# The exponentials of a graph attention kernel written twice by ScalarE: into PSUM for the weighting, into SBUF for the sums

## The chip, the cores and the metric

The kernel runs on one core of one Trainium2 chip. The metric is device time in microseconds (us). Three runs of the kernel before took 1232.32, 1234.52 and 1235.27 us; the median is 1234.52 us.

## What is computed

One graph attention layer with residual and layer norm, over 6250 nodes of 96 features, 4 heads of 24, and 106,250 edges (100,000 drawn ones in both directions and the self loops), sorted by destination. `src` plays the rows, `dst` the columns.

```python
q = (embeds[rows] @ qW).reshape(e, 4, 24)
k = (embeds[cols] @ kW).reshape(e, 4, 24)
v = (embeds[cols] @ vW).reshape(e, 4, 24)
exp_s = exp(clip(einsum('ehd,ehd->eh', q, k), -10, 10))
norms = segment_sum(exp_s, rows)[rows]
res = segment_sum(exp_s / (norms + 1e-8) * v, rows)
x = layernorm(x + x + res)
```

## The kernel before

**Set-up.** The nodes form 49 blocks of 128. x is transposed and multiplied by the three weights; k and v of every node go to a table in HBM (kv_table, 192 floats a row), q stays in SBUF (qt).

**Edges.** The edges are sorted by block on the chip, in 6 groups. After each group VectorE writes the list of table rows to gather (`dst_s`, line 1159) and the place of each edge in its block (`loc_s`). Sorted edges form 880 columns of 128, and five columns (U = 5) make a tile, so there are 176 tiles. Ten of them share their gathered rows in pairs, so GpSimd gathers for 171.

**A tile n** passes through these steps:
- GpSimd issues five indirect DMAs (line 511) that gather k and v into `kv`, a ring of eight buffers. Before a tile it waits until the ring's buffer is free (`s_wv` of tile n-8) and until the sums of tile n-6 are made (`s_res`).
- VectorE builds the one-hot matrix `ohb` (line 1191). TensorE transposes it ("t", line 679), ScalarE copies the transpose to `onehT` (line 776) and the matrix itself to `oneh` (line 782).
- TensorE multiplies `onehT` with q's block into the PSUM tensor `ps_q[n % 2]` ("q", line 653): q of each edge, 480 of 512 columns.
- VectorE multiplies with k ("prod", line 1202), reduces over 24 (line 1222) and clips (line 1230). ScalarE takes the exponential, 20 values a partition, into `wv[..., 96:100]` (line 769).
- VectorE multiplies v with these, each broadcast over 24, into `wv[..., 0:96]` ("wv", line 1212).
- TensorE multiplies `oneh` with the 100 columns of `wv` into `ps_r` ("r", line 667), and VectorE adds the five results to `acc` (line 1183): the weighted v and, in the last four columns, the sums of weights.

**Order.** A plan written at build time (`plan`) strings these steps together. Every engine walks it in the same order, one iteration m at a time, with work of several tiles in each, and each engine's queue is strictly in order. In iteration m:
- TensorE: q of tile m+1, r of tile m-1, t of tile m+2, then matmuls of the sort (a "unit" is 20 matmuls, line 636, one unit behind VectorE's, or the matmuls of a named piece, as `tally` at line 563 or `table` at lines 578 to 583).
- VectorE: prod of tile m, wv of tile m-1, then, once r of tile m-2 is there, the five additions of tile m-2, interleaved with reduce, build of tile m+2 and clip, then sort work.
- ScalarE: the first part of a unit's steps (line 728), the exponential of tile m, `onehT` of tile m+2, `oneh` of tile m+1 (after r of tile m-1), the other part of the steps.

Sort work of group g runs inside the iterations of group g-1's tiles. For each group VectorE ranks the edges first (`mark`, `tally`, `pair`, `count`, `base`, `bounds`, `select`, `table`, `tree`, with matmuls of tally, count and table between), then runs the units, and then a short end (`lower`, `differ`, `turn`, `choice`, `pick`), which crosses TensorE, ScalarE and VectorE several times. `pick` writes `dst_s`, for which GpSimd waits before the first tile of the group. After the last group there is no sort work. Then come the division, the residual, the layer norm and the stores.

**Waits that the change touches.** q of tile n waits for `onehT` of n and, since `ps_q` has two buffers, for prod of tile n-2:

```python
pe.wait_ge(s_oneT, n + 1)
wait(pe, s_prod, n - 1)
```

r of tile n waits for `wv` (`s_wv`), for `oneh` (`s_onf`) and for the additions of tile n-2.

Of the kernel before, what the change touches and what calls it, by code (L numbers as in the profile page):

```python
# [6 lines left out]
def gnn(nc, x, src, dst, qW, kW, vW, out):  # L7
# [3 lines left out]
    ACT = mybir.ActivationFunctionType  # L11
    AX = mybir.AxisListType

    P = 128
    N, D = x.shape
    E = src.shape[0]
    HEADS = 4
    DH = D // HEADS
# [4 lines left out]
    RW = D + HEADS  # L23
    U = 5
# [52 lines left out]
    def gathered(n):  # L77

        if not isinstance(n, int) or n >= MB + MT // U:
            return n - PAIRS // U  # L80
        return n if n < MB else MB + (n - MB) // 2
# [68 lines left out]
    with ExitStack() as ctx:  # L150
        def sb(name, shape, dt):
            return ctx.enter_context(nc.sbuf_tensor(name, shape, dt))

        def pb(name, shape, dt):
            return ctx.enter_context(nc.psum_tensor(name, shape, dt))

        def sem(name):
            return ctx.enter_context(nc.semaphore(name))
# [106 lines left out]
        clipped = sb("clipped", [P, 2, U * HEADS], f32)  # L265
        wv = sb("wv", [P, 2, U, RW], f32)
# [31 lines left out]
        ps_q = [pb(f"ps_q{i}", [P, 512], f32) for i in range(2)]  # L298
# [56 lines left out]
        s_prod = sem("s_prod")  # L355
        s_score = sem("s_score")
        s_clip = sem("s_clip")
        s_exp = sem("s_exp")
        s_wv = sem("s_wv")
        s_res = sem("s_res")  # L360
        s_acc = sem("s_acc")
# [12 lines left out]
        def wait(eng, s, v):  # L374

            if not (isinstance(v, int) and v <= 0):
                eng.wait_ge(s, v)
# [37 lines left out]
        def sums_of(g):  # L415

            return (ps_a, ps_b) if g == 0 else (ps_a[:, 0:256], ps_a[:, 256:512])

        def there(n):

            return not isinstance(n, int) or 0 <= n < NBT

        def blocks_of(engine, n):

            return nc.values_load_multi_w_load_instructions(  # L425
                blk_s[0:1, bass.ds(n * U, U)], engines=[engine], min_val=0, max_val=NB - 1,
                skip_runtime_bounds_check_because="clamped when the table is made")[1]
# [98 lines left out]
        def _(pe):  # L526
# [96 lines left out]
            def unit(g, v, vm):  # L623
                w = TS[g] + 1
                first = isinstance(v, int) and v == V0[g]
                last = isinstance(v, int) and v == V0[g + 1] - 1
                if first:
                    pe.wait_ge(s_blk, g + 1)
                pe.wait_ge(s_theta, v + 1)
                for to, lhs, s_made in zip(sums_of(g), (lhs_a, lhs_b), (s_lhs_a, s_lhs)):  # L630
                    pe.wait_ge(s_made, v + 1)
                    for j in range(SU):
                        steps = theta[:, vm, j, 0:w]
                        if j < (KG if g else KD):
                            steps = theta_g[:, vm, 0:w, j] if g else theta_d[:, vm, :, j]
                        mm = nc.tensor.matmul(to[:, 0:w], lhs[:, vm, :, j], steps,  # L636
                                              start=first and j == 0 and (g == 0 or lhs is lhs_a),
                                              stop=last and j == SU - 1 and (g == 0 or lhs is lhs_b))
                    if last and lhs is lhs_a:
                        mm.then_inc(s_half, 1)  # L640
                mm.then_inc(s_bin, 1)

            def tiles(m, mm, sorts, mid=()):
                n, nm = m + 1, (mm + 1) % R
                if there(n):

                    blks = blocks_of(mybir.EngineType.PE, n)
                    if isinstance(n, int) and n == 0:
                        pe.wait_ge(s_qi, NPC)
                    pe.wait_ge(s_oneT, n + 1)  # L650
                    wait(pe, s_prod, n - 1)
                    for u in range(U):
                        last = nc.tensor.matmul(ps_q[nm % 2][:, u * D:(u + 1) * D],  # L653
                                                onehT[:, nm % 2, u * P:(u + 1) * P],
                                                qt[:, bass.ds(blks[u], 1), :].rearrange("p a d -> p (a d)"),
                                                start=True, stop=True)
                    last.then_inc(s_q, 1)
                n, nm = m - 1, (mm - 1) % R
                if there(n):

                    pe.wait_ge(s_wv, n + 1)
                    pe.wait_ge(s_onf, n + 1)
                    wait(pe, s_acc, U * (n - 1))
                    for u in range(U):
                        final = isinstance(n, int) and n == NBT - 1
                        to = ps_last[u][:, 0:RW] if final else ps_r[nm % 2][:, u * RW:(u + 1) * RW]
                        last = nc.tensor.matmul(to, oneh[:, nm % 2, u, :], wv[:, nm % 2, u, :],  # L667
                                                start=True, stop=True)
                        if final:
                            last.then_inc(s_last, 1)  # L670
                    if not final:
                        last.then_inc(s_res, 1)
                n, nm = m + 2, (mm + 2) % R
                if there(n):

                    pe.wait_ge(s_one, n + 1)
                    wait(pe, s_oneT, n - 1)
                    for u in range(U):
                        last = nc.tensor.transpose(ps_t[nm % 2][:, u * P // 2:(u + 1) * P // 2].bitcast(bf16),  # L679
                                                   ohb[:, nm % 4, :, u], ident_bf[:, :])  # L680
                    last.then_inc(s_ot, 1)
                for piece, g in mid:
                    piece(g)
                for sort in sorts:
                    unit(*sort)
# [6 lines left out]
        def _(act):  # L692
# [70 lines left out]
            def tiles(m, mm, sorts, mid=()):  # L763
                if sorts:
                    unit(*sorts[0], halves=(0,))
                n, nm = m, mm
                if there(n):
                    act.wait_ge(s_clip, n + 1)
                    nc.scalar.activation(wv[:, nm % 2, :, D:RW],  # L769
                                         clipped[:, nm % 2, :].rearrange("p (u h) -> p u h", h=HEADS),  # L770
                                         ACT.Exp).then_inc(s_exp, 1)
                n, nm = m + 2, (mm + 2) % R
                if there(n):
                    wait(act, s_q, n - 1)
                    act.wait_ge(s_ot, n + 1)
                    nc.scalar.activation(onehT[:, nm % 2, :], ps_t[nm % 2][:, 0:U * P // 2].bitcast(bf16),  # L776
                                         ACT.Copy).then_inc(s_oneT, 1)
                n, nm = m + 1, (mm + 1) % R
                if there(n):
                    wait(act, s_res, n - 1)  # L780
                    act.wait_ge(s_one, n + 1)
                    nc.scalar.activation(oneh[:, nm % 2, :, :], ohb[:, nm % 4, :, :].rearrange("p n u -> p u n"),  # L782
                                         ACT.Copy).then_inc(s_onf, 1)
                if sorts:
                    unit(*sorts[0], halves=(1,))
                for piece, g in mid:
                    piece(g)
                for sort in sorts[1:]:
                    unit(*sort)
# [12 lines left out]
            for j, (a, b) in enumerate(PARTS):  # L802
                act.wait_ge(s_inv, j + 1)
                for i in range(a, min(b, NPC - 1)):
                    for k in range(PC if i < NPC - 2 else HALF):
                        if j + 1 < len(PARTS) and i == b - 1 and k == (PC - 2 if b < NPC - 2 else 2):
                            root(j + 1)
                        n = i * PC + k
# [6 lines left out]
        def _(dve):  # L815
# [356 lines left out]
            def tiles(m, mm, sorts, mid=()):  # L1172
# [33 lines left out]
                def weigh():  # L1206
                    n, nm = m - 1, (mm - 1) % R
                    if there(n):

                        km = (gathered(n) if isinstance(n, int) else nm - PAIRS // U) % R  # L1210
                        dve.wait_ge(s_exp, n + 1)
                        nc.vector.tensor_tensor(  # L1212
                            wv[:, nm % 2, :, 0:D].rearrange("p u (h d) -> p u h d", h=HEADS),
                            kv[:, km, :, D:2 * D].rearrange("p u (h d) -> p u h d", h=HEADS),
                            wv[:, nm % 2, :, D:RW].unsqueeze(3).to_broadcast([P, U, HEADS, DH]),
                            ALU.mult).then_inc(s_wv, 1)

                def reduce():
# [117 lines left out]
            for k in range(HALF, PC):  # L1336
                n = (NPC - 2) * PC + k
# [3 lines left out]
            n = (NPC - 1) * PC  # L1341
# [31 lines left out]
```

## Time and profile before

| what | us |
|---|---|
| median of three runs | 1234.52 |
| the profiled execution, own time | 1236.72 |
| its span, first to last instruction | 1234.9 |
| VectorE busy | 1036.8 (84%) |
| TensorE busy | 967.6 (78%) |
| GpSimd busy | 861.0 (70%) |
| ScalarE busy | 613.4 (50%) |

Busy time leaves out what an engine's sequencer does, such as issuing, waiting and branching. The column behind the bar in a row of costliest groups is the busy time and the mean of one; behind the second bar stands the idle time of that engine just before these instructions and what ended it. "Issue" means that the profile shows nothing that was waited for. In a timeline a row has its start, its duration, engine, line, operation and the tiles written and read; in brackets the idle time of the engine before it and what ended it. TensorE's granted clock was 0.754 of full speed on average.

### The profile page before, as it was taken

Reading aid. Unit: us, or ns where it says so; the run is one execution under the profiler, and the core shown is the slowest. Engines: PE = TensorE matmul, PEld = TensorE weight load, DVE = VectorE, ACT = ScalarE, POOL = GpSimd, SP = SyncE. Lnnn points to the kernel's source line nnn. Section 1 sums busy time; section 2 is a strip of 40 time slices with the busy share of each in tenths; the row PEclk is TensorE's granted clock in tenths of the full one; section 3 lists DMA queues with packets and bytes.
Section 4 is the critical chain, followed back from the end, with each engine's and each line's share of the span. In section 5 each row is a group of like instructions: output and inputs, shape, how many; then the busy total and the mean of one; then the engine's idle time right before and its main releaser. Section 6 shows DMA issues by size and latency. Waiting matters only on the chain.

```text
span 1234.9 us, 22885 instructions
## 1 busy us (share of the span) xinstructions
PE 967.6 (78%) x6512; PEld 881.1 (71%) x6513; DVE 1036.8 (84%) x3109; ACT 613.4 (50%) x1328; POOL 861.0 (70%) x888
## 2 busy tenths in 40 slices
PE   8875788688886888768998868978777788888770
PEld 6764777587775887667887767877677677777760
DVE  7989899999999999989999998999667855555557
ACT  6851583258732598323887323877333422222225
POOL 1207777777777777777777777777777777777752
PEclk9996597769976699865999855999767955555555
DMA  6202222223222222232222222222522222222222
GB/s 177 90 3 76 80 78 71 75 78 80 78 72 77 78 78 78 74 81 75 78 78 78 71 74 79 78 78 78 154 77 80 78 80 77 80 77 79 78 58 78
DMA packets 67240, 98.33 MB, mean 80 GB/s; under 512 B 33127, under 2 KB 53204, under 8 KB 67134
## 3 DMA queue, kind: packets, MB, share of 16 engines
q0 software_dynamic: 41040, 84.10, 25.1%
q1 hardware_dynamic: 26094, 12.94, 3.7%
q8 instruction: 51, 0.84, 0.3%
q14 instruction: 55, 0.45, 0.1%
HBM read 89.77 MB, written 7.22 MB: 79 GB/s over the span
## 4 chain that ended last, share of the span: by engine, by line
DVE 35%; POOL 22%; PE 18%; issue 17%; DVEq 4%; ACT 3%; DMA 0%; POOLq 0%; ACTq 0%
POOL kv L511 22%; DVE acc L1183 7%; PE ps_r L667 5%; PE ps_q L653 4%; DVE place_m L1119 4%; DVEq L425 4%; DVE prod L1202 3%; DVE place_m L1123 3%; DVE wv L1212 3%; PE ps_a L636 2%; DVE steps_m L872 1%; PE ps_t L679 1%; PE ps_a L563 1%; DVE place_m L1071 1%; PE ps_r L548 1%
## 5 line engine op out<-in xcount | busy, mean ns | idle before, releaser
L511 POOL DMA_INDIRECT kv<-kv_table,dst_s x855 | 840.0, 982 | 306.9 <-issue 299.0
L653 PE MATMUL ps_q<-qt,onehT 128*128 x1760 | 319.2, 347 | 99.5 <-ACT onehT L776 95.5
L667 PE MATMUL ps_r<-wv,oneh 128*128 128x100 f32 x1752 | 325.7, 352 | 90.9 <-DVE wv L1212 90.2
L653 PEld LDWEIGHTS ps_q<-qt,onehT 128*128 128x128 f32 x1760 | 291.5, 254 | 123.5 <-issue 123.4
L667 PEld LDWEIGHTS ps_r<-wv,oneh 128*128 128x128 f32 x1752 | 296.2, 259 | 112.1 <-DVE wv L1212 109.5
L728 ACT ACTIVATE steps_m<-iota_f,pos_t 125x254 f16<-125x254 f32 (+4 forms) x652 | 255.8, 479 | 13.1 <-PE ps_b L636 8.8
L1183 DVE TENSOR_TENSOR acc<-acc,ps_r 128x100 f32 x876 | 221.9, 253 | 41.9 <-issue 12.9
L776 ACT ACTIVATE onehT<-ps_t 128x640 f32<-128x640 bf16 x176 | 123.8, 704 | 209.3 <-PE ps_t L679 202.1
L769 ACT ACTIVATE wv<-clipped 128x20 f32<-128x20 f32 x176 | 38.5, 219 | 344.6 <-DVE clipped L1230 340.0
L1202 DVE TENSOR_TENSOR prod<-ps_q,kv 128x480 f32<-128x480 f32 x176 | 114.9, 653 | 111.2 <-DMA kv<-kv_table,dst_s 100.7
L782 ACT ACTIVATE oneh<-ohb 128x640 f32<-128x640 bf16 x176 | 164.2, 933 | 0.8 <-PE ps_r L667 0.8
L636 PE MATMUL ps_a<-steps_m,place_m 125*128 125x254 f16 (+4 forms) x1220 | 152.8, 268 | 0.0
L636 PEld LDWEIGHTS ps_a<-steps_m,place_m 125*128 125x128 f16 x1220 | 134.0, 139 | 1.9
L1222 DVE TENSOR_REDUCE score<-prod 128x20 f32<-128x480 f32 x176 | 113.9, 647 | 4.9 <-PE ps_r L667 2.5
L1212 DVE TENSOR_TENSOR wv<-kv,wv 128x480 f32<-128x480 f32 x176 | 114.3, 650 | 2.5 <-issue 2.2
L679 PE MATMUL ps_t<-ident_bf,ohb 128*128 128x128 bf16 x880 | 103.1, 264 | 8.8 <-DVE ohb L1191 8.2
L679 PEld LDWEIGHTS ps_t<-ident_bf,ohb 128*128 128x128 bf16 x880 | 87.0, 138 | 18.7 <-DVE ohb L1191 17.4
L1191 DVE TENSOR_TENSOR ohb<-iota_t,loc_s 128x640 bf16<-128x640 bf16 x176 | 97.6, 554 | 0.0
L636 PE MATMUL ps_a<-theta_g,place_m 125*128 125x254 f16 (+3 forms) x284 | 56.5, 280 | 16.8 <-ACT steps_m L728 16.8
L1123 DVE TENSOR_TENSOR place_m<-place_m,ps_b 125x1280 f16<-125x1280 f16 x71 | 57.8, 815 | 0.2
L1126 DVE TENSOR_TENSOR place_m<-place_m,ps_b 125x1280 f16<-125x1280 f16 x71 | 57.8, 814 | 0.0
L1119 DVE TENSOR_TENSOR place_m<-iota_s,ps_b 125x1280 f16<-125x1280 f16 x71 | 57.8, 814 | 0.0
(214 smaller groups left out, 691.2 us busy)
## 6 DMA issues: line engine op xcount, KB each, us to landing
kv<-kv_table,dst_s POOLq DMA_INDIRECT x855
kv_table<-kv SPq DMA_DIRECT2D x7, 672.0 KB, 3.4
acc<-in_x_dram SPq DMA_DIRECT2D x6, 336.0 KB, 6.6
steps_m<-in_x_dram SPq DMA_DIRECT2D x6, 336.0 KB, 5.3
out_dram<-kv SPq DMA_DIRECT2D x6, 336.0 KB
dst_i<-in_dst_dram SPq DMA_DIRECT2D x1, 415.0 KB
src_i<-in_src_dram SPq DMA_DIRECT2D x1, 346.7 KB
acc<-in_x_dram SPq DMA_DIRECT2D x1, 288.0 KB, 4.4
```

What stands on the lines that cost most here:

```text
L511: nc.gpsimd.indirect_dma_start(kv[:, nm, u, :], None, kv_dram, bass.IndirectOffsetOnAxis(ap=dst_s[:, n * U + u:n * U + u + 1], axis=0)).th ...
L636: mm = nc.tensor.matmul(to[:, 0:w], lhs[:, vm, :, j], steps, start=first and j == 0 and (g == 0 or lhs is lhs_a), stop=last and j == SU - ...
L653: last = nc.tensor.matmul(ps_q[nm % 2][:, u * D:(u + 1) * D], onehT[:, nm % 2, u * P:(u + 1) * P], qt[:, bass.ds(blks[u], 1), :].rearrange ...
L667: last = nc.tensor.matmul(to, oneh[:, nm % 2, u, :], wv[:, nm % 2, u, :], start=True, stop=True)
L679: last = nc.tensor.transpose(ps_t[nm % 2][:, u * P // 2:(u + 1) * P // 2].bitcast(bf16), ohb[:, nm % 4, :, u], ident_bf[:, :])
L728: last = nc.scalar.activation(theta[:, vm, j, 0:w], iota_f[0:EP, 0:w], ACT.Sign, scale=-1.0, bias=pos_t[:, bass.ds(v * SU + j, 1)])
L776: nc.scalar.activation(onehT[:, nm % 2, :], ps_t[nm % 2][:, 0:U * P // 2].bitcast(bf16), ACT.Copy).then_inc(s_oneT, 1)
L782: nc.scalar.activation(oneh[:, nm % 2, :, :], ohb[:, nm % 4, :, :].rearrange("p n u -> p u n"), ACT.Copy).then_inc(s_onf, 1)
L1183: nc.vector.tensor_tensor(at, at, from_ps, ALU.add).then_inc(s_acc, 1)
L1202: nc.vector.tensor_tensor(prod[:, nm % 2, :].rearrange("p (u d) -> p u d", u=U), ps_q[nm % 2][:, 0:U * D].rearrange("p (u d) -> p u d", u= ...
L1212: nc.vector.tensor_tensor(wv[:, nm % 2, :, 0:D].rearrange("p u (h d) -> p u h d", h=HEADS), kv[:, km, :, D:2 * D].rearrange("p u (h d) -> ...
L1222: nc.vector.tensor_reduce(score[:, nm % 2, :], prod[:, nm % 2, :].rearrange("p (h d) -> p h d", d=DH), axis=AX.X, op=ALU.add).then_inc(s_s ...
```

## The change

ScalarE's exponential now writes 20 values a partition into the 32 spare columns of the tile's own `ps_q` buffer, and VectorE's weighting reads them there. A second exponential of the same clipped scores, placed on ScalarE's queue behind the copy to `onehT`, writes `wv[..., 96:100]` as before and has its own semaphore `s_sum`. As the weights lie in the buffer that q of tile n+2 overwrites, q of tile n no longer waits for prod of tile n-2 but for wv of tile n-2. r waits for `s_sum` too.

```diff
+        def weights(nm):
+
+            return ps_q[nm % 2][:, U * D:U * D + U * HEADS].rearrange("p (u h) -> p u h", h=HEADS)
...
                     pe.wait_ge(s_oneT, n + 1)
-                    wait(pe, s_prod, n - 1)
+                    wait(pe, s_wv, n - 1)
...
                     pe.wait_ge(s_wv, n + 1)
+                    pe.wait_ge(s_sum, n + 1)
                     pe.wait_ge(s_onf, n + 1)
...
                     act.wait_ge(s_clip, n + 1)
-                    nc.scalar.activation(wv[:, nm % 2, :, D:RW],
+                    nc.scalar.activation(weights(nm),
                                          clipped[:, nm % 2, :].rearrange("p (u h) -> p u h", h=HEADS),
                                          ACT.Exp).then_inc(s_exp, 1)
...
                     nc.scalar.activation(onehT[:, nm % 2, :], ps_t[nm % 2][:, 0:U * P // 2].bitcast(bf16),
                                          ACT.Copy).then_inc(s_oneT, 1)
+                n, nm = m, mm
+                if there(n):
+                    nc.scalar.activation(wv[:, nm % 2, :, D:RW],
+                                         clipped[:, nm % 2, :].rearrange("p (u h) -> p u h", h=HEADS),
+                                         ACT.Exp).then_inc(s_sum, 1)
...
                             kv[:, km, :, D:2 * D].rearrange("p u (h d) -> p u h d", h=HEADS),
-                            wv[:, nm % 2, :, D:RW].unsqueeze(3).to_broadcast([P, U, HEADS, DH]),
+                            weights(nm).unsqueeze(3).to_broadcast([P, U, HEADS, DH]),
                             ALU.mult).then_inc(s_wv, 1)
```

## Rows read from the trace of the kernel before

**Rows 1.** The page, costliest groups: gather, prod, wv, exponential.

```profile
L511 POOL DMA_INDIRECT kv<-kv_table,dst_s x855 | 840.0, 982 | 306.9 <-issue 299.0
L1202 DVE TENSOR_TENSOR prod<-ps_q,kv 128x480 f32<-128x480 f32 x176 | 114.9, 653 | 111.2 <-DMA kv<-kv_table,dst_s 100.7
L1212 DVE TENSOR_TENSOR wv<-kv,wv 128x480 f32<-128x480 f32 x176 | 114.3, 650 | 2.5 <-issue 2.2
L769 ACT ACTIVATE wv<-clipped 128x20 f32<-128x20 f32 x176 | 38.5, 219 | 344.6 <-DVE clipped L1230 340.0
```

**Rows 2.** Instructions of tile dst_s: shortest, median, longest in ns; first, last start.

```profile
L511 POOL DMA_INDIRECT kv<-kv_table,dst_s x855: 940/946/2863, 90.0 to 1194.2; - x171
```

**Rows 3.** Timeline of GpSimd: gathers of tiles 17, 39 and 50.

```profile
202.24 0.94 POOL L511 DMA_INDIRECT kv<-kv_table,dst_s  x1 [2.88 <-DVE dst_s L1159]
...
345.61 1.09 POOL L511 DMA_INDIRECT kv<-kv_table,dst_s  x1 [2.21 <-PE ps_r L667]
...
417.26 0.94 POOL L511 DMA_INDIRECT kv<-kv_table,dst_s  x1 [0.82 <-issue]
```

**Rows 4.** Timeline of GpSimd and VectorE: gathers begun while VectorE works.

```profile
112.44 1.09 POOL L511 DMA_INDIRECT kv<-kv_table,dst_s  x1 [0.30 <-issue]
...
273.08 0.81 DVE L1126 TENSOR_TENSOR place_m<-place_m,ps_b 125x1280 f16<-125x1280 f16 x1
...
273.58 0.94 POOL L511 DMA_INDIRECT kv<-kv_table,dst_s  x1 [0.30 <-issue]
...
723.28 0.65 DVE L1212 TENSOR_TENSOR wv<-kv,wv 128x480 f32<-128x480 f32 x1
723.42 1.32 POOL L511 DMA_INDIRECT kv<-kv_table,dst_s  x1 [0.30 <-issue]
...
1102.39 1.02 POOL L511 DMA_INDIRECT kv<-kv_table,dst_s  x1 [0.30 <-issue]
```

**Rows 5.** Timeline at the table of group 1: q, wv, r, then VectorE's read.

```profile
124.81 2.45 PE L653 MATMUL ps_q<-qt,onehT 128*128 x10 [0.94 <-ACT onehT L776]
...
127.03 0.65 DVE L1212 TENSOR_TENSOR wv<-kv,wv 128x480 f32<-128x480 f32 x1
127.73 2.46 PE L667 MATMUL ps_r<-wv,oneh 128*128 128x100 f32 x10 [0.48 <-DVE wv L1212]
...
131.36 0.26 DVE L997 CAST blk_s<-ps_a 1x110 int32<-1x110 f32 x1 [2.38 <-PE ps_a L583]
```

**Rows 6.** The same read of groups 2 and 4.

```profile
253.90 0.28 DVE L997 CAST blk_s<-ps_a 1x125 int32<-1x125 f32 x1
...
570.08 0.31 DVE L997 CAST blk_s<-ps_a 1x160 int32<-1x160 f32 x1 [0.75 <-PE ps_a L583]
```

**Rows 7.** Timeline at the last unit of group 1.

```profile
187.02 1.36 PE L667 MATMUL ps_r<-wv,oneh 128*128 128x100 f32 x10 [0.94 <-DVE wv L1212]
...
188.39 0.47 PE L679 MATMUL ps_t<-ident_bf,ohb 128*128 128x128 bf16 x5
...
192.38 0.40 PE L636 MATMUL ps_a<-theta_g,place_m 125*128 125x205 f16 x2 [1.70 <-ACT steps_m L728]
...
195.61 0.66 DVE L1202 TENSOR_TENSOR prod<-ps_q,kv 128x480 f32<-128x480 f32 x1
```

**Rows 8.** Timeline: VectorE at the start of group 1's units.

```profile
149.41 0.37 DVE L1115 TENSOR_TENSOR theta_g<-iota_g,ps_b 125x410 f16<-125x410 f16 x1 [1.45 <-PE ps_a L636]
```

**Rows 9.** Timeline: prod of tile 64, behind the tally of group 4.

```profile
527.15 0.66 DVE L1202 TENSOR_TENSOR prod<-ps_q,kv 128x480 f32<-128x480 f32 x1 [1.44 <-PE ps_q L653]
```

**Rows 10.** Timeline: r of tile 70, and the gather of tile 76.

```profile
580.56 2.46 PE L667 MATMUL ps_r<-wv,oneh 128*128 128x100 f32 x10 [0.85 <-DVE wv L1212]
...
585.51 0.95 POOL L511 DMA_INDIRECT kv<-kv_table,dst_s  x1 [0.30 <-issue]
```

**Rows 11.** Timeline after the last group: q of tile 146, prod of tile 145.

```profile
1005.89 2.45 PE L653 MATMUL ps_q<-qt,onehT 128*128 x10 [0.88 <-ACT onehT L776]
...
1006.81 0.66 DVE L1202 TENSOR_TENSOR prod<-ps_q,kv 128x480 f32<-128x480 f32 x1 [1.98 <-DMA kv<-kv_table,dst_s]
```

More of the change, by code:

```diff
@@ L358, in gnn @@
         s_exp = sem("s_exp")
+        s_sum = sem("s_sum")
         s_wv = sem("s_wv")
```

## The prediction

> **What bounds the kernel now.** Read the page's costliest groups first: VectorE has the most busy time, but GpSimd's 855 gathers have 840.0 us busy and 299.0 us idle put down to issue [rows 1], 1139 us in a span of 1234.9. The tile view says that they run from 90.0 to 1194.2 us [rows 2]: 1104 us over 855 is 1.29 us each, and one alone takes 0.946 (median) and 0.30 of issue, 1.25. So GpSimd is never idle for long, and the end comes with its last gather. Then read GpSimd's timeline for every pause above 0.30 us. After 90 us there are three [rows 3]: at 202.24 for the sorted list of group 1 (from VectorE), at 345.61 and at 417.26 for r of the tile six before (from TensorE). So GpSimd sets the time, but VectorE's sort and TensorE's r come just in time up to 417 us: what delays them there delays GpSimd. Behind the last group VectorE waits for gathers instead [rows 11].
>
> **The part that gains: wv no longer has two inputs in SBUF.** 855 x (982 - 946) ns = 31 us of the gathers is lengthening [rows 1, 2]. Look at what VectorE did when a long one began: wv started at 723.28, a gather at 723.42, wv ended at 723.93 and the gather 0.81 us later, at 724.74 [rows 4]. All 52 gathers that begin well inside a wv are lengthened so; of 202 that begin inside prod, the reduction or the unit's products, which have at most one SBUF input, 201 are not, as the one inside line 1126 with its PSUM operand [rows 4]. Counting the ones that a wv lengthens by over 15 ns gives 57, first at 112.44 and last at 1102.39 [rows 4], together 10.1 us, of which 4.8 us after 585 us. This goes. (The building of ohb does the same, 11.4 us, and stays.) [...]
>
> **wv's own duration.** No row shows wv with weights in PSUM. Nearest is prod, same size with one PSUM input: 653 ns against 650 [rows 1]. Bounds: 176 x 3 ns = +0.5 us, and at best the few tens of ns by which VectorE itself waits when a gather began first, -1 us. I take 0.
> [...]
>
> **The exponential.** The one into PSUM replaces one of 219 ns [rows 1]. ScalarE writes no PSUM in the trace, so the bounds are 0 and the 933 ns of its longest regular copy; VectorE's wait before wv is 2.5 us in all [rows 1], and wv follows prod, so nothing shows at either but the high end. I take 219. The second costs 176 x 219 ns = 38.5 us of ScalarE, which idles 344.6 us before exponentials alone: 0, except where `oneh` behind it is urgent (below). s_sum comes before the next q starts, so r never waits for it.
>
> **The part that costs: q waits for wv of two tiles before.** Today q of tile m+1 runs far ahead, during VectorE's previous iteration: q at 124.81, while the wv that it will have to follow is at 127.03 and ends at 127.68 [rows 5]. [...] q itself still comes in time for its prod. What is late next, place by place up to 585 us:
> - Table. VectorE waits at 131.36 for matmuls that follow wv, r, t without a gap, 2.38 us idle already [rows 5]: +2.45. There are four such places, groups 1 to 4, the second and the last in [rows 6]; at the second VectorE is just not idle, so up to 0.1 less. 9.7 us.
> - First units of group 1: VectorE waits 1.45 us for TensorE's units [rows 8], and these follow r. The clock rises inside them, so between 1.3 and 2.0; I take 1.4.
> - Last unit of groups 1, 2, 3: r 187.02, t 188.39, onehT, oneh, five steps on ScalarE, units 192.38, then q, on which prod at 195.61 waits [rows 7]. It is one unbroken chain: +1.27 for q and +0.22 for the second exponential ahead of oneh. 3 x 1.49 = 4.5 us.
> - Tally of group 4: prod of tile 64 already waits 1.44 us for a q that stands behind the tally [rows 9], and the tally behind r: +2.4.
> - The ends of the groups and the other iterations: q is still there before its prod, and r before its additions. 0.
>
> VectorE is then 9.7 + 1.4 + 4.5 + 2.4 = 18.0 us late at 585 us.
> GpSimd: its first gather of tile 76 starts at 585.51, and the one before ended at 585.21 [rows 10]. It needs r of tile 70, which ended at 580.56 + 2.46 = 583.02 [rows 10], 2.2 us earlier; a wait for r ends some 0.5 us behind the modelled end (as before 417.26), so 1.7 us are spare. r moves by VectorE's 18.0 and by q's 2.45 in front of it: 18.0 + 2.45 - 1.7 = +18.8 us for GpSimd. What the freed port gave before that is lost, since GpSimd waits here anyway; so is a lower sum at the earlier places (tile 17: 2.45 + 1.4 + 1.49 = 5.3; tile 50: 5.3 + 3.8 + 2.4 + 2.45 = 14). Behind 585 us there is no pause for GpSimd to the end, and the lists of groups 4 and 5 come well ahead of their first gather: only the port counts, -4.8.
> Behind the last group the order costs nothing: TensorE's round q, r, t, copy, q takes 6.1 to 6.3 us, it waits 0.88 in it for the copy, and prod waits 1.98 us for its gather [rows 11]; only the phase moves.
>
> **Sum.** Against the profiled execution, 1236.72 us of its own (span 1234.9, 1.8 around it): 1236.7 + 18.8 - 4.8 = 1250.7. That execution lies 2.2 above the median 1234.52, so 1248.5; I say 1248. Ends: the four table places may cost 1.3 each where the clock is at its upper level, and r the same, 6 us less; each place where TensorE has spare time that I did not see takes 1 to 2 off; on the other side the skipped ends of groups (4 of them at 1 to 1.5) and a dearer wv add 6. Own range 1239 to 1256.
>
> **Rivals.**
> - The port gain carries through: q is early by microseconds today, so its new wait costs nothing, and all 10.1 us go from a bound engine: 1224. For it: GpSimd is busy throughout [rows 2], and q starts before wv in every row. Against: what counts is not q, but r and the table behind it [rows 5]. Not slower; it decides if TensorE has 2.5 us spare behind wv. 7%.
> - Partly absorbed: a VectorE delay of 18 us is taken up by spare time, the first pauses [rows 3] cost about 5 us and the port gives 5 back: 1235. For it: VectorE idles 2.38, 1.45 and 1.44 us at these very places. Against: it idles because of TensorE, so this idle time moves along. 10%.
> - [...] 11%.
> - That the change does not do what it says (r or the sums waiting elsewhere) I see no way for.
>
> **From cases to numbers.** Main case 72%: 1248. A difference of 0.3%, 3.7 us, is what a measurement of this kernel can tell from none. Faster by more: 8% (the first rival and a rest). Within: 10%. Slower: 82%. The range for 8 in 10 takes the main case's and part of the second and third rival: 1236 to 1258.
>
> **What would show it.** In the trace after: gathers inside a wv at 0.95 us; q's matmuls starting within 0.1 us behind wv, TensorE's waits for wv in front of q and no longer in front of r; VectorE's idle time before the table's read near 4.8 us for group 1; GpSimd's pauses in front of tiles 17, 24 to 28, 39, 45 to 51 and 71 to 76, some 19 us more in all; wv at 650 ns. I am wrong if r follows wv at once, if those pauses are missing, or if wv is above 700 ns.

## The result, and the profile after

The changed kernel takes 1248.96 us (median of 5 runs, 1246.27 to 1250.0) where the kernel before, on the same chip, took 1235.27 (5 runs): a ratio of 1.012, 95% interval 1.010 to 1.014. So it is 14 us slower; 1248 was forecast. The profiled execution took 1248.96 us of its own, span 1247.1.

The groups of the page after, in the columns of [rows 1]:

```profile
L516 POOL DMA_INDIRECT kv<-kv_table,dst_s x855 | 827.3, 968 | 332.6 <-issue 320.2
L658 PE MATMUL ps_q<-qt,onehT 128*128 x1760 | 318.9, 345 | 245.4 <-DVE wv L1223 211.1
...
L673 PE MATMUL ps_r<-wv,oneh 128*128 128x100 f32 x1752 | 309.7, 342 | 2.6 <-DVE wv L1223 2.6
...
L1213 DVE TENSOR_TENSOR prod<-ps_q,kv 128x480 f32<-128x480 f32 x176 | 114.8, 652 | 105.8 <-DMA kv<-kv_table,dst_s 91.5
...
L775 ACT ACTIVATE ps_q<-clipped 128x20 f32<-128x20 f32 x176 | 32.7, 186 | 169.2 <-DVE clipped L1241 169.0
L1223 DVE TENSOR_TENSOR wv<-kv,ps_q 128x480 f32<-128x480 f32 x176 | 113.3, 644 | 2.6 <-issue 2.2
```

Read it against [rows 1]. The gathers got shorter, 968 ns from 982, which is 12.7 us less busy time, but GpSimd's idle time grew by more. TensorE's 211.1 us of waiting for wv now stands in front of q; before, 90.2 us of it stood in front of r (row below). Now r waits 2.6 us in all, because what it needs is there by the time that q has passed. wv takes 644 ns.

```profile
L667 PE MATMUL ps_r<-wv,oneh 128*128 128x100 f32 x1752 | 325.7, 352 | 90.9 <-DVE wv L1212 90.2
```

GpSimd's tile view [rows 2] says what that makes at the end: the last gather starts 12.3 us later, though the first starts 0.8 us earlier.

```profile
L516 POOL DMA_INDIRECT kv<-kv_table,dst_s x855: 940/946/2142, 89.2 to 1206.5; - x171
```

What the text calls the port gain is only this: wv no longer lengthens gathers. No run shows a port; the word is the author's name for the effect. In the timeline after, a gather that starts inside a wv takes 0.95 us, where [rows 4] had 1.02 to 1.32.

```profile
111.27 0.64 DVE L1223 TENSOR_TENSOR wv<-kv,ps_q 128x480 f32<-128x480 f32 x1
111.65 0.95 POOL L516 DMA_INDIRECT kv<-kv_table,dst_s  x1 [0.30 <-issue]
```

The table of group 1, against [rows 5]: q starts 0.25 us behind wv's end (within 0.1 was forecast), not before wv, r comes 2.2 us after q's start, and VectorE's idle time before its read has gone from 2.38 to 4.70.

```profile
126.16 0.64 DVE L1223 TENSOR_TENSOR wv<-kv,ps_q 128x480 f32<-128x480 f32 x1
...
127.05 2.44 PE L658 MATMUL ps_q<-qt,onehT 128*128 x10 [1.78 <-DVE wv L1223]
...
129.28 2.35 PE L673 MATMUL ps_r<-wv,oneh 128*128 128x100 f32 x10
...
132.79 0.26 DVE L1008 CAST blk_s<-ps_a 1x110 int32<-1x110 f32 x1 [4.70 <-PE ps_a L588]
```

And GpSimd's pauses. Before there were three [rows 3]; now there are 21, the last in front of tile 76. Some of them, in GpSimd's timeline (the number in brackets is the pause):

```profile
172.66 0.94 POOL L516 DMA_INDIRECT kv<-kv_table,dst_s  x1 [1.15 <-issue]
...
186.98 0.94 POOL L516 DMA_INDIRECT kv<-kv_table,dst_s  x1 [2.11 <-issue]
...
204.84 0.94 POOL L516 DMA_INDIRECT kv<-kv_table,dst_s  x1 [5.67 <-DVE dst_s L1170]
...
352.76 1.09 POOL L516 DMA_INDIRECT kv<-kv_table,dst_s  x1 [2.34 <-PE ps_r L673]
...
422.98 1.06 POOL L516 DMA_INDIRECT kv<-kv_table,dst_s  x1 [2.82 <-issue]
...
569.66 0.94 POOL L516 DMA_INDIRECT kv<-kv_table,dst_s  x1 [2.51 <-issue]
...
603.93 0.94 POOL L516 DMA_INDIRECT kv<-kv_table,dst_s  x1 [0.91 <-issue]
```

**One balance for all kernels.** GpSimd's queue holds little but gathers, so the start of the last one is the start of the first, plus their busy time, plus the pauses, plus the 0.30 us in front of each gather (259 us in every kernel). This is bookkeeping: it tells where the time went, not why. The table has these for every kernel, from its profiled execution ("pauses": what is above 0.30 us in every pause over 0.33, after the first gather). Each is one execution: e4's was the fastest of its 12, e6's the slowest of its 12 (1239.4 us against a median of 1234.8). Before to after: -0.8 of start, -12.7 of busy, +25.9 of pauses make +12.4, and +12.3 was measured. The last column is the median over the median before on the same chip.

| kernel | pauses | gathers busy | last gather at | ratio, 95% interval |
|---|---|---|---|---|
| before | 5.0 | 840.0 | 1194.2 | |
| after | 30.9 | 827.3 | 1206.5 | 1.012, 1.010 to 1.014 |
| e1, order only | 23.1 | 838.2 | 1210.7 | 1.0115, 1.0092 to 1.0138 |
| e2, other bank | 8.8 | 827.8 | 1186.3 | 0.9937, 0.9922 to 0.9952 |
| e2 again | 8.7 | 826.0 | 1184.4 | 0.9935, 0.9921 to 0.9949 |
| e3, r ahead of q | 39.3 | 825.6 | 1214.3 | 1.0183, 1.0166 to 1.0200 |
| e4, table ahead of q | 13.4 | 829.9 | 1192.1 | 1.0020, 1.0007 to 1.0034 |
| e6, unread weights in PSUM | 9.4 | 838.6 | 1196.8 | 0.9992, 0.9978 to 1.0006 |
| e8, other bank, table early | 1.8 | 830.7 | 1181.3 | 0.9919, 0.9889 to 0.9949 |

### The profile page after: what moved, and what is told of

Read it like the earlier page. It is cut to its first block, busy times and chain, and to the rows that moved or that the text cites. A ratio compares the mean times of both kernels' runs of the same rounds, so it can differ in the third digit from the quotient of the medians.

```text
span 1247.1 us, 23223 instructions
## 1 busy us (share of the span) xinstructions
PE 924.1 (74%) x6512; PEld 859.8 (69%) x6513; DVE 1034.7 (83%) x3109; ACT 621.1 (50%) x1504; POOL 848.3 (68%) x888
## 4 chain that ended last, share of the span: by engine, by line
DVE 33%; PE 25%; issue 16%; POOL 15%; ACT 5%; DVEq 4%; DMA 1%; SPq 0%; POOLq 0%; ACTq 0%
POOL kv L516 15%; PE ps_q L658 8%; DVE acc L1194 7%; PE ps_r L673 6%; DVEq L430 4%; DVE place_m L1130 3%; DVE wv L1223 3%; DVE prod L1213 3%; PE ps_a L641 3%; DVE place_m L1134 3%; ACT steps_m L734 2%; PE ps_t L685 2%; DVE steps_m L883 1%; PE ps_a L568 1%; ACT oneh L793 1%
## 5 line engine op out<-in xcount | busy, mean ns | idle before, releaser
L516 POOL DMA_INDIRECT kv<-kv_table,dst_s x855 | 827.3, 968 | 332.6 <-issue 320.2
L658 PE MATMUL ps_q<-qt,onehT 128*128 x1760 | 318.9, 345 | 245.4 <-DVE wv L1223 211.1
L658 PEld LDWEIGHTS ps_q<-qt,onehT 128*128 128x128 f32 x1760 | 286.4, 250 | 278.1 <-issue 277.7
L673 PE MATMUL ps_r<-wv,oneh 128*128 128x100 f32 x1752 | 309.7, 342 | 2.6 <-DVE wv L1223 2.6
L775 ACT ACTIVATE ps_q<-clipped 128x20 f32<-128x20 f32 x176 | 32.7, 186 | 169.2 <-DVE clipped L1241 169.0
L1223 DVE TENSOR_TENSOR wv<-kv,ps_q 128x480 f32<-128x480 f32 x176 | 113.3, 644 | 2.6 <-issue 2.2
L685 PE MATMUL ps_t<-ident_bf,ohb 128*128 128x128 bf16 x880 | 96.3, 252 | 5.1 <-DVE ohb L1202 5.1
```

The costliest lines, as they stand in the source:

```text
L516: nc.gpsimd.indirect_dma_start(kv[:, nm, u, :], None, kv_dram, bass.IndirectOffsetOnAxis(ap=dst_s[:, n * U + u:n * U + u + 1], axis=0)).th ...
L1223: nc.vector.tensor_tensor(wv[:, nm % 2, :, 0:D].rearrange("p u (h d) -> p u h d", h=HEADS), kv[:, km, :, D:2 * D].rearrange("p u (h d) -> ...
```

## The experiments

The theory: two effects that have nothing to do with each other, the port gain (weights in PSUM) and a loss on TensorE's queue (q waits for wv, and what is behind q waits too). The rivals: the second exponential or the PSUM write matters by itself; or q's own lateness costs, not what stands behind it. e1 to e4 ran on one chip (before: 1237.65 us there), e6, e8 and "e2 again" on another occasion (before: 1235.7).

**e1, the loss alone.** The kernel before with the new wait and nothing else.

```diff
-                    wait(pe, s_prod, n - 1)
+                    wait(pe, s_wv, n - 1)
```

> The kernel before with one edit: q of a tile waits for wv of the tile two before instead of its prod. Weights stay in SBUF, one exponential. Theory (the new wait costs, the freed port gives back): the whole delay without what the port gives back after 585 us and without the second exponential in front of oneh (3 x 0.22), so before + 18 to 19, about 1253. Rival 1 (the second exponential, or the one into PSUM, on ScalarE's queue is what makes things late): no loss from this edit, 1235. Rival 2 (the freed port gives nothing, the delay alone is 13): 1248, the same as the changed kernel.

Measured: 1252.54 us (1247.02 to 1257.03), ratio 1.0115. In the timeline the table's wait is there, and the gathers are still lengthened by wv (67 of them, 12.7 us):

```profile
133.15 0.26 DVE L997 CAST blk_s<-ps_a 1x110 int32<-1x110 f32 x1 [3.85 <-PE ps_a L583]
...
209.77 0.65 DVE L1212 TENSOR_TENSOR wv<-kv,wv 128x480 f32<-128x480 f32 x1
209.81 1.43 POOL L511 DMA_INDIRECT kv<-kv_table,dst_s  x1 [0.30 <-issue]
```

The last gather starts 16.5 us later than before. So one changed wait makes the whole loss. Without the port gain e1 should be slower than the changed kernel. Its last gather is 4.2 us later, but that is one execution each, and e1's own runs lie within 10 us of each other; the two intervals of the ratio overlap. So the times do not show this part; the lengthened gathers do, 67 against none.

**e2, the gain alone.** Both exponentials and the weights in PSUM, but in spare columns of a `ps_t` buffer that q does not write, so that q waits for prod as before.

```diff
+            return ps_t[(nm + 1) % 2][:, U * P // 2:U * P // 2 + U * HEADS].rearrange("p (u h) -> p u h", h=HEADS)
...
-                    nc.scalar.activation(wv[:, nm % 2, :, D:RW],
+                    nc.scalar.activation(weights(nm),
```

> The changed kernel with the weights in PSUM, but in spare columns of the other transpose bank, ps_t of tile n+1, which is idle between the copy to onehT of n+1 and the transposes of n+3. So q waits for prod again as in the kernel before; both exponentials stay. Theory: no delay from order; the port's gain counts only where GpSimd is not held by VectorE, behind the pause at 417 us: about 6 us of the 10.1, so 1229; gathers inside wv at 0.95 us. Rival 1 (ScalarE's exponentials cost): 1248 or near. Rival 2 (the port gives nothing): 1235.

Measured: 1229.14 us (1227.92 to 1231.91), ratio 0.9937; the second time ("e2 again") 1227.71 against 1235.7, 0.9935. That run stood on record with this:

> The other-bank kernel once more, beside the two others on one chip: the ratio to before is 0.9937 as the first time, within 0.002. If the port gain is all of it, its ratio and that of the kernel with the unread weights in PSUM differ by 0.006 to 0.007; if the gain has another origin, they agree.

```profile
112.52 0.65 DVE L1223 TENSOR_TENSOR wv<-kv,ps_t 128x480 f32<-128x480 f32 x1
112.90 0.95 POOL L516 DMA_INDIRECT kv<-kv_table,dst_s  x1 [0.30 <-issue]
...
131.74 0.26 DVE L1008 CAST blk_s<-ps_a 1x110 int32<-1x110 f32 x1 [2.38 <-PE ps_a L588]
```

The table's idle time is that of before, 2.38, and no gather inside a wv is lengthened. What is gained comes late: the gather of tile 90 starts 0.2 us earlier than before, that of tile 108 5.6 us, the last 7.9. Up to tile 64 GpSimd is held up by VectorE and TensorE here and there, and a shorter gather only makes the next pause longer (5.0 to 8.8 us). Not all of the 7.9 is the lengthening by wv, which had 4.8 us behind tile 76. Another 3.0 come from other gathers that this trace has shorter there: before, a few of them began inside VectorE's ranking for the next group (3.3 us of lengthening behind tile 76, 0.2 in e2). The longest gather before is one of them:

```profile
688.76 0.63 DVE L872 TENSOR_SCALAR steps_m<-bin_u 125x160 f16<-125x160 uint16 x5
688.92 2.86 POOL L511 DMA_INDIRECT kv<-kv_table,dst_s  x1 [0.30 <-issue]
```

**e3, r ahead of q.** The changed kernel with the two blocks of TensorE exchanged.

```diff
 tiles(m, mm, sorts, mid=()) of TensorE, after:
-  q of m+1 (waits for wv of m-1), r of m-1, t of m+2, pieces, units
+  r of m-1, q of m+1 (waits for wv of m-1), t of m+2, pieces, units
```

> The changed kernel with r in front of q on TensorE's queue (r, q, t instead of q, r, t). VectorE's delay stays, since table, tally and units still stand behind both; r itself is no longer behind q, so GpSimd's wait for r of six tiles before ends up to 2.45 us sooner. Theory: peak delay of GpSimd 16.4 instead of 18.5, and 2 us less at the end: 1246.5 to 1247. Rival (r behind q is the whole cost, and the sort's delays are absorbed): 1235 to 1238.

Measured: 1259.17 us (1256.74 to 1263.23), ratio 1.0183. My expectation was wrong, by 12 us and in its sign. The waits of e3 (us in total, times, longest), where the changed kernel has 13.6 us in 13 waits:

```profile
DVE prod L1213 <- PE ps_q L674: 61.5, 46, 2.6
```

I had thought of q as early with room to spare. It is not, once it must follow wv: q of tile m+1 then has what is left of VectorE's iteration, and r (2.46 us where the granted clock is 0.50) in front of it uses that up, so that prod waits 46 times (up to tile 72, 16 times and 18.5 us in all, against 8 times and 6.8 us in the changed kernel). VectorE is 28.5 us later than before at tile 72, where the changed kernel is 17.8 later. With this wait, q first is the better of the two orders: the loss is not that of a badly placed r, but of everything waiting for wv at once.

**e4, the table ahead of q.** The changed kernel, but in the iterations that hold a table TensorE's order is r, t, table, q.

```diff
+                if any(piece is table for piece, g in mid):
+                    r_of()
+                    t_of()
+                    pieces()
+                    q_of()
+                else:
+                    q_of()
...
```

> The changed kernel with q behind the table's matmuls in the iterations that hold the table of a group (five of them, order r, t, table, q), else unchanged. Theory: VectorE's reads of the table come 2.45 us sooner in each of four groups, but q is then late for the next prod by 0.3 to 0.8 in three of them: 8 us less, 1241. Rival (the delay comes from r alone, or from the units' ends): 1248.

Measured: 1239.97 us (1234.51 to 1242.91), ratio 1.002. 1241 was expected. The profiled execution lies 5.5 us under the median of these runs, so its row in the balance flatters it by some 5 us. Its timeline at the table of group 1:

```profile
126.93 2.13 PE L675 MATMUL ps_r<-wv,oneh 128*128 128x100 f32 x10 [2.34 <-DVE wv L1238]
...
129.93 0.26 PE L588 MATMUL ps_a<-coef,after 49*128 49x2 f16 x4
130.12 2.45 PE L659 MATMUL ps_q<-qt,onehT 128*128 x10
130.23 0.26 DVE L1023 CAST blk_s<-ps_a 1x110 int32<-1x110 f32 x1 [2.05 <-PE ps_a L588]
```

So the order in these few iterations alone brings the loss from 13.7 us (1248.96 - 1235.27) to 2.3 (1239.97 - 1237.65). That is more than the 8.1 us that the table reads cost in the changed kernel; the next section has the rest.

**e6, weights in PSUM that nobody reads.** As e2 in every instruction, but the first exponential goes to `wv`, from where the weighting reads it, and the second to the spare PSUM columns.

```diff
                     nc.scalar.activation(wv[:, nm % 2, :, D:RW],
...
+                    nc.scalar.activation(weights(nm),
+                                         clipped[:, nm % 2, :].rearrange("p (u h) -> p u h", h=HEADS),
+                                         ACT.Exp).then_inc(s_sum, 1)
```

> The order of before is kept, and both exponentials are there: the first goes into wv in SBUF, which the weighting reads as before, the second goes into the spare columns of the other bank of ps_t, where nobody reads it. Theory (the gain of the other-bank kernel comes only from the weighting having one input in PSUM): the weighting again lengthens the gathers that start inside it, near 57 of them and 10 us in all, and the time is that of before within 0.4% (near 1237 on the chip where before took 1237.65). Rival 1 (the gain came from the second exponential, which gives r its own wait, or from the shift of ScalarE's work): near 1229 to 1231. Rival 2 (the second exponential costs something on ScalarE that the port gain has covered so far): 1240 or more. Gathers lengthened by the weighting tell: zero in the first kernel of this kind, near 57 here.

Measured: 1234.81 us (1231.14 to 1239.4), ratio 0.9992, no change; e2 beside it had 0.9935. Of 66 gathers that start inside a wv and over 0.15 us before its end, 65 are lengthened (e2 again: none of 69):

```profile
152.01 0.65 DVE L1223 TENSOR_TENSOR wv<-kv,wv 128x480 f32<-128x480 f32 x1
152.17 1.30 POOL L516 DMA_INDIRECT kv<-kv_table,dst_s  x1 [0.30 <-issue]
```

So the second exponential is free and brings nothing, and the gain comes from the place from which the weighting reads: partly at once, through the gathers that wv no longer lengthens, partly (see e2) through where the other gathers then fall.

**e8, the two lessons together.** e2, and in the iterations that hold a table TensorE issues q (which still waits for prod only), the table, then r and t.

```diff
+                early = any(piece is table for piece, g in mid)
+                q_of()
+                if early:
+                    pieces()
+                r_of()
+                t_of()
+                if not early:
+                    pieces()
```

> The other-bank kernel, and in the six iterations that hold a table, TensorE issues q, the table's pieces, then r and t. Theory (VectorE's idle before the table reads, 2.38, 1.18, 0.75 and 2.43 us in groups 1, 3, 4 and 5, ends when the table of TensorE is ready, and part of it reaches GpSimd): these idles fall to 0 to 0.3 us, the pauses of GpSimd behind dst_s shrink, and the time is 1226 where the other-bank kernel takes 1229, 2 to 3 us less. Rival 1 (VectorE's lateness before tile 96 is made up by slack before the end): 1229, no change. Rival 2 (r, now behind the table, delays r's reader and the accumulation, and q's buffer is unaffected): 1230 to 1232.

Measured: 1223.66 us (1222.07 to 1232.28), ratio 0.9919. It has the lowest median of all, 12 us under the kernel before. It is 4.0 us under e2 on the same chip (2 to 3 were expected), but two of its six runs took 1231.5 and 1232.3 us, and its interval, 0.9889 to 0.9949, overlaps that of e2: that it beats e2 is not shown by the times. The trace shows that the tables come earlier, in five iterations (the sixth table, of group 0, is read at 37 us, before the first tile).

```profile
126.48 0.64 DVE L1236 TENSOR_TENSOR wv<-kv,ps_t 128x480 f32<-128x480 f32 x1
126.58 0.32 PE L583 MATMUL ps_a<-wafter,weigh_h 49*128 49x163 f16 x1
...
127.17 2.45 PE L675 MATMUL ps_r<-wv,oneh 128*128 128x100 f32 x10
128.34 0.25 DVE L1021 CAST blk_s<-ps_a 1x110 int32<-1x110 f32 x1
```

The table's matmuls run in the time in which TensorE waited for wv anyway, r starts right behind wv all the same, and VectorE reads without a pause in all the groups. GpSimd's pauses shrink to 1.8 us, so now the shorter gathers count from the start.

## Why the prediction was right

**The mechanism and the total were right; several terms were not.** To see the terms, take the start of prod of every tile, after minus before, and sum the steps from tile 0 to tile 70, by place. That is VectorE's lateness; the forecast was 18.0 us. The same for e1 and e4 (each number rounded by itself):

| place | forecast | after | e1 | e4 |
|---|---|---|---|---|
| four table reads | 9.7 | 8.1 | 8.5 | 0.1 |
| first units of group 1 | 1.4 | -0.5 | 3.3 | -0.1 |
| last units of groups 1 to 3 | 4.5 | 3.6 | 3.3 | 3.7 |
| tally of group 4 | 2.4 | 1.1 | -1.3 | -1.2 |
| ends of groups 1 to 3 | 0 | 3.6 | 2.2 | -2.0 |
| iterations amid the units of groups 2 and 3 | 0 | 2.9 | 2.5 | 2.6 |
| rest | 0 | -0.1 | 0 | -0.3 |
| sum | 18.0 | 18.7 | 18.6 | 2.7 |

- **q's duration.** The forecast moves what stands behind q by 2.45 us, or by 1.27. These are q's durations in the kernel before: 2.45 where the granted clock is 0.50 [rows 5], 1.27 where it is 1.00 (q at 184.81 us). In the changed kernel TensorE waits 1.78 us for wv in front of q at 127.05, q takes 2.44 at 0.50, and r comes behind it.
- **Table reads.** Right for groups 1 and 2 (idle time +2.32 and +2.33 us in front of the read, 2.45 and 2.35 forecast). In groups 3 and 4 it was +1.88 and +1.46: mis-sized by 1.6 in all.
- **First units of group 1.** The sign was wrong. TensorE's clock rose earlier than before (last section), and what follows took half the time (r 1.28 us instead of 2.35).
- **Last units.** Right in kind: three steps of 1.2 us, 1.49 forecast. The timeline shows where, at the first read of the finished sums, for which VectorE waits 1.10, 1.33 and 1.54 us, and at most 0.35 before.
- **Tally.** 1.1 us against 2.4: prod of tile 64 waits 1.72 us for q, only 0.28 more than in [rows 9].
- **"The ends of the groups and the other iterations: 0" is the step that failed.** Its reason was that q is still there before its prod; it is not. It is worth 6.5 us. At the end of group 2, for one, prod of tile 39 waits 1.86 us for q (0.45 before), and in groups 2 and 3 a unit's product waits 0.41 to 0.56 us for TensorE five times. The errors of the other terms, 5.7 us the other way, hid it: the sum is right partly by luck.

VectorE's timeline after, in this order: last unit of group 1, unit of group 2, prod of tile 39, prod of tile 64.

```profile
197.19 0.37 DVE L1145 TENSOR_TENSOR dif<-cum_a 128x204 f16<-128x204 f32 x1 [1.10 <-ACT cum_a L758]
...
291.27 0.39 DVE L1126 TENSOR_TENSOR theta_g<-iota_g,ps_b 125x450 f16<-125x450 f16 x1 [0.41 <-PE ps_a L641]
...
374.82 0.66 DVE L1213 TENSOR_TENSOR prod<-ps_q,kv 128x480 f32<-128x480 f32 x1 [1.86 <-PE ps_q L658]
...
543.52 0.66 DVE L1213 TENSOR_TENSOR prod<-ps_q,kv 128x480 f32<-128x480 f32 x1 [1.72 <-PE ps_q L658]
```

e4 shows also that the places are not independent. It frees the table reads (8.0 us), and the ends of groups and the tally then cost 7.9 us less too. Nor do e1 and the changed kernel split alike: they come to the same sum by different terms. How late TensorE is there depends on how the work before has fallen; why the ends come out even below those of before I have not settled.

**From VectorE to GpSimd.** The gather of tile 76 starts 18.4 us later, 18.8 were forecast. There is no pause after it, as forecast. On the way the forecast was too high: 2.6 us for 5.3 at tile 17, 12.7 for 14 at tile 50. The forecast of the pauses contradicted itself: "some 19 us more" left out the port gain of the first half, which the pauses had to swallow. They grew by 25.9. I had also missed the pauses at tiles 13 and 15 (172.66 and 186.98, 2.7 us) and at 63 and 64 (2.0 us).

**The give-back.** From tile 76 to the last gather 6.1 us come back, 4.8 forecast. Gathers lengthened by wv went from 58 (10.6 us; the prediction counts 57 and 10.1) to none, and the 4.8 us of them behind tile 76 came back as forecast. The 1.3 us more were not foreseen; they come from where the other gathers fell. Over the whole kernel, gathers that begin inside the building of ohb were lengthened by 12.6 us before and 14.7 after; the remaining lengthened ones by 8.1 before and 4.2 after (7.8 in e6, 7.9 in e8). Every one of these, 28 before and 29 after, begins inside another VectorE instruction, above all the ranking's comparisons (line 872: 3.8 us before, 1.6 after) and its scans (line 1050: 2.5 and 1.0). The prediction had no term for a change in these. The balance by terms: 18.4 - 6.1 = 12.3 at the last gather, 14.0 forecast.

**wv and the exponential.** wv takes 644 ns against 650 [rows 1], so 0 was a fair value. The upper end of the forecast's range counts a dearer wv in its 6 us. No run shows one: with weights in PSUM wv takes 644 ns in e2 and 642 in e8 too. The exponential into PSUM takes 186 ns, 33 less than the 219 that I took; the second takes 211 ns with no wait of its own.

**The rivals.** "The port gain carries through" is refuted as forecast, but e2 shows where it would have been right: with another bank, q keeps its old wait, and some 8 us come. "Partly absorbed" is refuted: VectorE has made up nothing by tile 75, where prod still starts 18.8 us later. The third rival, at 11%, had TensorE become the bound inside units because the granted clock is at its lower level for some iterations more, each at 3 us: 1260 in all. That was the author's estimate, and no run shows the 3 us. The iterations amid the units of groups 2 and 3 cost 2.9 us instead of 12. A longer stay at the lower level did appear: in group 1's units the granted clock was 0.57 from 167 to 171 us and 0.58 from 181 to 185, where it was 1.00 before. But the steps there are no larger than in e1, whose clock was 1.00 in both stretches: 1.2 against 1.1 us at the last unit.

## What to carry to other kernels

In these traces r, t and the sort's matmuls never passed a q that stood waiting in front of them (in the changed kernel r at 129.28 follows q at 127.05, though the wv that both need ended at 126.80). So before an instruction gets a later wait, list what stands behind it in the queue, not only who reads its result. Two tensors in one bank's buffer share its release, so put a small operand where its release is already late enough. And if the bound engine pauses anywhere, a gain on it counts only behind its last pause; add up start, busy and pauses of that engine, and you see where its end comes from (here to 0.3 us), then look for the cause of each.

## What the runs showed of the hardware

- **Gathers inside the weighting.** The weighting with both inputs in SBUF lengthens a gather that starts inside it, over 0.15 us before its end, in 54 of 58, 64 of 66 and 65 of 66 cases (before, e1, e6), up to 1.44 us from 0.946. The lengthened gather ends 0.82 us behind wv, so one that starts later than that loses nothing. In all seven exceptions the gather began in wv's first 0.03 us, and it was wv that took longer, 0.71 to 0.72 us instead of 0.65. With one input in PSUM it is none of 64, 72 and 70 (after, e2, e8). The size, the instruction and its output are the same. What differs is where one input lies. Two SBUF inputs are not the only case: of 19 gathers that begin inside a comparison of line 872, which has one, 11 are lengthened (before).
- **ScalarE writes 20 elements a partition to PSUM faster than to SBUF**: as the first of the two, 186 (after) or 191 ns (e2) against 219 (before, e6); as the second, 186 (e6) against 211 (after, e2).
- **TensorE's clock rose at another time, and a term went from -0.5 to 3.3 us.** Below is the table by windows, first of the kernel before, then of the changed one (columns: stretch, length, busy us of PE, PEld, DVE, ACT and POOL with the number of instructions, TensorE's granted clock, DMA share, GB/s).

```profile
142.00:148.00 6.00, 6.00 (x34) 5.92 (x34) 5.91 (x15) 4.42 (x12) 4.78 (x5) 0.50 0.32 84
148.00:154.00 6.00, 5.12 (x49) 4.85 (x48) 4.55 (x9) 6.00 (x17) 4.48 (x6) 0.97 0.29 76
```

```profile
142.00:148.00 6.00, 4.90 (x43) 4.75 (x43) 5.95 (x17) 3.79 (x10) 4.50 (x5) 0.88 0.31 83
```

At 0.50 r takes 2.35 us and VectorE waits 1.45 us for the unit [rows 8]. In the changed kernel the clock is at its upper level some 5 us earlier (0.88 on average in the stretch where it was 0.50), though TensorE had been less busy in the 6 us before (2.49 us against 3.32), r takes 1.28 us, and VectorE waits 0.27. In e1 the clock is still at 0.60 in the second of these stretches, and VectorE waits 3.93 us at that place. What starts the rise at one time or another was not tried. The same new wait costs 3.3 us there in e1 and gives 0.5 in the changed kernel.
